# A fourth attention with four step banks, an opening in eight banks, and routed rows ranked before the router's turn

## The chip, the cores and the metric

The kernel runs on one core of one Trainium2 chip. The metric is the device time of one execution in microseconds. The kernel is written by hand for the five engines (TensorE, VectorE, ScalarE, GpSimd, SyncE); each has its own program, and they meet at semaphores.

## The reference

Four layers, each a cross attention and a feed-forward part, over `x` (16 batches of 100 tokens, 256 wide) with a context of 361 rows of 192 for every batch, all in float32:

```python
x = x + tanh(g_xattn[0]) * L0_xattn(ctx, layernorm(x), mask, ...)   # 4 heads of 64; keys and values of context and latents; q and k RMS-normed
x = x + tanh(g_ffn[0])   * L0_ffn(layernorm(x), ...)                # top-1 of 8 experts, 256 -> 2x1024 -> 256
x = x + tanh(g_xattn[1]) * L1_xattn(layernorm(x), ctx, ...)         # 8 heads of 64
x = x + tanh(g_ffn[1])   * L1_ffn(layernorm(x), ...)
x = x + tanh(g_xattn[2]) * L2_xattn(layernorm(x), ctx, ...)         # 4 heads of 64
x = x + tanh(g_ffn[2])   * L2_ffn(layernorm(x), ...)
x = x + tanh(g_xattn[3]) * L3_xattn(layernorm(x), ctx, ...)         # one head of 256, layer norms on both sides
x = x + tanh(g_ffn[3])   * L3_ffn(layernorm(x), ...)                # slots
```

The router of the first feed-forward picks one expert for every row: the kernel counts each row's rank among the rows of its expert, writes the rows to memory sorted by expert, and runs 20 tiles of 128 rows.

## The kernel before

The work goes in phases, attention and feed-forward in turn; within an attention the batches are pipelined. Every engine's program lists the same steps by hand in its own order, and an engine works strictly in that order.

PSUM has eight banks of 512 columns. In an attention, `S_bank` (banks 0, 1) takes scores, `PT_bank` (2, 3) the probabilities turned, `O_bank` (4) their products with the values, `R_bank` (5) the output turned, its projection and the router's small products, and `J_bank` (6, 7) the steps that prepare a later batch: turns and projections of context and x. A step is a group of matmuls by TensorE into a bank (raising `proj`), and a copy of the bank into SBUF by ScalarE (raising `copied`). TensorE's step n waits until the copy of the step two places before is done, since that one used the same bank.

**First attention (L = 0).** Twelve steps a batch. 0 and 1 turn the context's norms, 2 turns x, (5, 6) and (7, 11) are pairs that project the context to keys and values, 4 and 3 project x, 8 and 9 turn the keys and 10 the queries. 8, 9 and 10 need the keys and queries scaled by their root mean square: VectorE sums the squares (L1615, L1619, function `rms`), GpSimd takes the power and multiplies (L928, L933), five blocks a batch. Before the loop the opening prepares batches 0 and 1: batch 0's nine steps of `ALONE`, then those of batch 1 mixed with 8, 9, 10 of batch 0. `order_of` numbers these steps, `parity_of` gives the bank of two. ScalarE copies in that order, as its own list says. Then `first_attend(t)` runs for every batch, with steps for t+1 and t+2 between its own scores, turns and products. In it TensorE calls `o_turn(t-1)` (turn of the output, then `router_turn` of t-2), later `pair_blocks` of the pair (5, 6) of t+2, then the turns of the probabilities (`probs_turn`), and `project(t-1)` (projection, router logits, and `router_ranks` of t-3: two products, one for the ranks within the batch, L2348, one for the counts, L2349). VectorE reads ranks and counts in `residual` after `out`.

**Fourth attention (L = 3).** One head; four steps a batch: 0 turns x, 1 and 2 turn the context's two halves, 3 projects x. They alternate over banks 6 and 7; scores and probabilities alternate over banks 0, 1 and 2, 3 by batch. `fourth_attend(t)` on TensorE: scores of t, `o_turn(t-1)`, steps 0, 1, 2 of t+1, `project(t-1)` with the turn of the mixture's norms of t-2 (L2355), `probs_turn(t)`, step 3 of t+1, `weigh(t)`. ScalarE: `o_copy(t-1)` (L1129), copy of step 0 (L1061), exponential of t (L1118), copies of 1, 2 (L1065) and 3 (L1069). VectorE: maximum of t (L1637), statistics of x of t+2, copy of the turned probabilities (L1646), residual of t-1, x norm of t+2, `o_scale(t)` (L1656), norm for the mixture. SyncE loads the context norms of a batch twice (288 KB each), with the slot weights of the last phase between.

Lines of TensorE: L2444 context turn and L2442 the same in the fourth attention, L2450 x turn, L2406 and L2414 the two parts of a pair, L2456 projections of x, L2473 and L2476 turns of keys and queries, L2522 and L2518 scores, L2533 turns of the probabilities, L2554 products with the values, L2563 output turn, L2573 projection, L2334 router turn. L1073 is ScalarE's copy of steps 0 and 1 in the first attention, L1575 VectorE's context norm.

## Time and profile before

| | us |
|---|---|
| time, median of 3 runs | 1630.54 |
| lowest, highest | 1622.14, 1632.22 |
| the profiled execution's own time | 1626.69 |
| its span, first to last instruction | 1624.8 |
| TensorE busy | 1497.7 (92%) |
| TensorE weight load busy | 1087.5 (67%) |
| VectorE busy | 898.7 (55%) |
| ScalarE busy | 606.4 (37%) |
| GpSimd busy | 291.1 (18%) |

The profile is of one execution. PE is TensorE's matmul, PEld its weight load, DVE is VectorE, ACT ScalarE, POOL GpSimd, SP SyncE. A row of the timeline may merge equal instructions that follow each other (x4); its second number is the time from the first one's start to the last one's end. In brackets stands the idle time of the engine just before, and what ended it. Neighbouring matmuls overlap a little. PEclk is the granted TensorE clock, 1.00 for 2.4 GHz and 0.50 for 1.2.

### The profile page before, as it was taken

Reading aid. Unit: us, or ns where it says so; the run is one execution under the profiler, and the core shown is the slowest. Engines: PE = TensorE matmul, PEld = TensorE weight load, DVE = VectorE, ACT = ScalarE, POOL = GpSimd, SP = SyncE. Lnnn points to the kernel's source line nnn. Section 1 sums busy time; section 2 is a strip of 40 time slices with the busy share of each in tenths; the row PEclk is TensorE's granted clock in tenths of the full one; section 3 lists DMA queues with packets and bytes.
Section 4 is the critical chain, followed back from the end, with each engine's and each line's share of the span. In section 5 each row is a group of like instructions: output and inputs, shape, how many; then the busy total and the mean of one; then the engine's idle time right before and its main releaser. Section 6 shows DMA issues by size and latency. Waiting matters only on the chain.

```text
span 1624.8 us, 30316 instructions
## 1 busy us (share of the span) xinstructions
PE 1497.7 (92%) x9070; PEld 1087.5 (67%) x9070; DVE 898.7 (55%) x2901; ACT 606.4 (37%) x1704; POOL 291.1 (18%) x409
## 2 busy tenths in 40 slices
PE   5999999869999989999999989979999899878897
PEld 2566666559999956777677766747777644556665
DVE  4788788642222224555445444556666556556776
ACT  3655555412223323444434424304434100454342
POOL 4555556430000040000000000110000001121000
PEclk9999999959999999999999999989999899999898
DMA  5111114338999940000000000011100100243001
GB/s 138 32 34 37 36 36 155 118 122 299 324 329 320 327 127 15 20 18 18 18 9 18 10 1 10 17 41 30 37 27 27 33 13 20 65 148 100 1 11 31
DMA packets 89654, 128.85 MB, mean 79 GB/s; under 512 B 17362, under 2 KB 74786, under 8 KB 84450
## 3 DMA queue, kind: packets, MB, share of 16 engines
q1 hardware_dynamic: 85954, 123.50, 23.7%
q0 software_dynamic: 2432, 4.34, 0.9%
q8 instruction: 39, 0.64, 0.2%
q14 instruction: 45, 0.37, 0.1%
q10 hardware_dynamic: 1184, 0.01, 0.0%
HBM read 112.87 MB, written 11.67 MB: 77 GB/s over the span
## 4 chain that ended last, share of the span: by engine, by line
PE 75%; issue 8%; DVE 7%; POOL 3%; DMA 3%; ACT 3%; SPq 1%; ACTq 0%; POOLq 0%; DVEq 0%
PE bank L2406 10%; PE bank L2554 9%; PE bank L2763 7%; PE bank L2414 6%; PE bank L2856 6%; PE bank L2522 5%; PE bank L2533 4%; PE bank L2573 4%; PE bank L2777 4%; PE bank L2809 3%; PE bank L2825 3%; PE bank L2495 2%; PE bank L3007 2%; DMA work<-in_F_b1c 1%; PE bank L2456 1%
## 5 line engine op out<-in xcount | busy, mean ns | idle before, releaser
L1646 DVE COPY work<-bank 128x300 f32<-128x300 f32 (+1 forms) x272 | 124.0, 489 | 144.5 <-PE bank L2533 143.2
L2554 PEld LDWEIGHTS bank<-work 128*100 128x100 f32 x1760 | 177.1, 171 | 34.0 <-issue 19.1
L2554 PE MATMUL bank<-work 128*100 128x64 f32 (+1 forms) x1760 | 191.5, 260 | 9.1 <-DVE work L1646 7.2
L1118 ACT ACTIVATE work<-bank,work 100x361 f32<-100x361 f32 (+1 forms) x272 | 158.7, 590 | 52.3 <-DVE work L1637 36.2
L1981 DVE SCALAR_TENSOR_TENSOR work<-bank,work 128x128 f32<-128x128 f32 x160 | 56.1, 350 | 160.4 <-PE bank L2763 148.5
L2763 PE MATMUL bank<-work 128*128 128x128 f32 x1216 | 142.7, 275 | 0.7 <-DMA work<-in_F_b1c 0.5
L2763 PEld LDWEIGHTS bank<-work 128*128 128x128 f32 x1216 | 140.5, 192 | 2.2 <-ACT work L1239 1.2
L1637 DVE TENSOR_REDUCE work<-bank 100x1 f32<-100x361 f32 x208 | 102.0, 528 | 68.7 <-PE bank L2522 66.1
L2533 PEld LDWEIGHTS bank<-ident,work 100*128 100x128 f32 x880 | 91.7, 144 | 43.0 <-issue 22.8
L2533 PE MATMUL bank<-ident,work 100*128 100x100 f32 x880 | 107.3, 256 | 7.1 <-ACT work L1118 6.6
L1239 ACT ACTIVATE work<-bank,work 128x128 f32<-128x128 f32 x160 | 58.7, 367 | 143.7 <-PE bank L2763 138.7
L2522 PE MATMUL bank<-work 64*100 64x361 f32 (+1 forms) x512 | 110.2, 508 | 0.6 <-ACT work L1102 0.6
L1108 ACT COPY work<-bank 128x512 f32<-128x512 f32 (+2 forms) x96 | 41.3, 482 | 154.0 <-PE bank L2414 154.0
L906 POOL TENSOR_TENSOR work<-work,neg_half 100x1 f32<-100x1 f32 x64 | 35.2, 550 | 331.1 <-DVE work L1595 296.2
L2856 PE MATMUL bank<-F_weight,work 128*128 128x512 f32 (+1 forms) x208 | 92.3, 603 | 0.0
L928 POOL TENSOR_TENSOR work<-work,neg_half 128x4 f32<-128x4 f32 x80 | 82.0, 1024 | 42.2 <-DVE work L1619 42.1
L865 POOL TENSOR_TENSOR work<-work,neg_half 100x1 f32<-100x1 f32 x48 | 28.1, 586 | 296.3 <-DVE work L1503 270.2
L1105 ACT COPY work<-bank 128x361 f32<-128x361 f32 x96 | 39.5, 464 | 96.5 <-PE bank L2414 96.5
L2777 PE MATMUL bank<-work 128*128 128x256 f32 x320 | 72.5, 380 | 0.5 <-DVE work L1981 0.5
L2856 PEld LDWEIGHTS bank<-F_weight,work 128*128 128x128 f32 (+1 forms) x208 | 39.1, 190 | 49.0 <-issue 39.7
L2777 PEld LDWEIGHTS bank<-work 128*128 128x128 f32 x320 | 59.3, 190 | 7.8 <-DVE work L1981 0.7
L2406 PE MATMUL bank<-L_WkvT,work 128*128 128x512 f32 (+1 forms) x128 | 50.6, 518 | 14.2 <-ACT work L1073 13.5
(390 smaller groups left out, 2754.5 us busy)
## 6 DMA issues: line engine op xcount, KB each, us to landing
work<-in_F_w SPq DMA_DIRECT2D x58, 1024.0 KB, 5.7
work<-in_ctxT SPq DMA_DIRECT2D x64, 180.5 KB, 2.4
work<-context_norms SPq DMA_DIRECT2D x32, 288.0 KB, 3.5
context_norms<-work SPq DMA_DIRECT2D x16, 288.0 KB, 2.5
work<-in_ctx SPq DMA_DIRECT2D x16, 192.0 KB, 2.9
work<-in_F_b SPq DMA_DIRECT2D x20, 128.0 KB, 6.4
work<-sorted_x SPq DMA_DIRECT2D x20, 128.0 KB, 2.6
sorted_y<-work SPq DMA_DIRECT2D x20, 128.0 KB, 5.9
```

The lines of the kernel that those rows point to most:

```text
L928: nc.gpsimd.tensor_tensor(rr[j][:, 4 * k:4 * k + 4], rr[j][:, 4 * k:4 * k + 4], neg_half[:, 0:4], ALU.pow).then_inc(s.rqk.sem, 1)
L1118: nc.scalar.activation(pr[:, 0:NK], S_bank[k][0:T, 0:NK], ACT.Exp, bias=nmax[k][0:T, :], accum_out=rsum[j][0:T, h:h + 1]).then_inc(s.exped ...
L1637: nc.vector.tensor_reduce(nmax[k][0:T, :], S_bank[k][0:T, 0:NK], axis=AXX, op=ALU.max, negate=True).then_inc(s.maxed.sem, 1)
L1646: nc.vector.tensor_copy(PT[k][:, 0:CH, :], PT_bank[k][:, 0:CH * T].rearrange("p (c t) -> p c t", c=CH)).then_inc(s.probs_copied.sem, 1)
L2406: nc.tensor.matmul(to, lhs, rhs, start=(i == 0), stop=False, skip_group_check=True)
L2414: ins = nc.tensor.matmul(to, lhs, rhs, start=False, stop=True, skip_group_check=True)
L2522: ins = nc.tensor.matmul(S_bank[k][0:T, 0:NK], QT[j][b:b + W, m, :], kt(L, j)[b:b + W, m, 0:NK], start=True, stop=True)
L2533: ins = nc.tensor.transpose(PT_bank[k][:, c * T:(c + 1) * T], PR[k][0:T, c, :], ident[0:T, 0:T])
L2554: ins = nc.tensor.matmul(to, PT[k][:, c, :], values, start=(c == 0), stop=(c == CH - 1))
L2763: ins = nc.tensor.matmul(bank[to + f % 2][:, 0:P], first_weights(i, j)[:, c, col:col + P], TT[j][:, c, :], start=(c == 0), stop=(c == 1))
L2777: ins = nc.tensor.matmul(bank[6 + j][:, 0:D], AC[j][:, f, :], W2[j][:, f, :], start=(f == 0), stop=(f == HID0 // P - 1))
L2856: ins = nc.tensor.matmul(bank[3 + q % Y_BANKS][0:k, :], GXT[:, c, i * P:i * P + k], lin2[:, c, 2 * g:2 * g + 2, :].rearrange("p e n -> p ( ...
```

## The change

Three parts.

The opening's nineteen steps are listed in `OPENING`, in their order; step k goes to bank (6 + k) mod 8, and waits for the copy seven places before. TensorE turns x of batch 0 before the first pair, and batch 1's context between the projections of batch 0's x. Two steps of the opening, the pair (7, 11) of batch 1, keep their places and banks 7 and 6.

In the fourth attention the steps 0 to 3 have banks 6, 7, 1 and 3; scores are always in bank 0 and turned probabilities in bank 2. A step waits only for the copy of the same step of the batch before. Step 1 of t+1 goes ahead of `o_turn(t-1)`, so ScalarE's copy of step 0 waits for the first two steps.

`router_ranks` goes from the end of `project` into `o_turn`, ahead of `router_turn`.

```diff
+OPENING = ((0, 0), (0, 1), (0, 2), (0, 5), (0, 6), (0, 4), (1, 0), (1, 1), (0, 3), (0, 7), (0, 11), (1, 2), (1, 5), (1, 6),
+           (0, 8), (1, 4), (1, 3), (0, 9), (0, 10))
...
+def opens(t, n):
+
+    return isinstance(t, int) and (t, n) in OPENING
+
+
+def reused_after(t, n):
+
+    return order_of(t, n) - (7 if opens(t, n) else 1)
+
+
 def order_of(t, n):
 
+    if opens(t, n):
+        return OPENING.index((t, n))
...
+        def ahead_bank(t, n):
+            return bank[(6 + order_of(t, n)) % 8] if opens(t, n) else J_bank[parity_of(t, n)]
...
             if L == 3 and isinstance(t, int) and t == 0:
                 return S_bank[n % 2]
+            if L == 3:
+                return (bank[6], bank[7], bank[1], bank[3])[n]
...
                         src = step_bank(L, t, j, n)
-                        wait_for(act, s.proj, STEPS[L] * t + place_of(L, t, n) + 1)
+                        wait_for(act, s.proj, STEPS[L] * t + (2 if L == 3 and n < 2 else place_of(L, t, n) + 1))
...
-                    for n in ALONE:
-                        step(0, 0, n)
                     act.wait_ge(loaded["head_gains"], 16 * n_loads["head_gains"])
...
-                    for n in AHEAD[:-2]:
-                        step(*((0, 0) if n in OF_NEXT else (1, 1)), n)
+                    for t, n in OPENING:
+                        step(t, t, n)
...
-                        wait_for(pe, s.copied, STEPS[L] * t + place - 1)
+                        if L == 3 and not (isinstance(t, int) and t == 0):
+                            wait_for(pe, s.copied, STEPS[L] * (t - 1) + n + 1)
+                        else:
+                            wait_for(pe, s.copied, STEPS[L] * t + place - 1)
...
                     if PAIRS[L] == 0:
-                        wait_for(pe, s.exped, n - 1)
+                        wait_for(pe, s.exped, n)
...
-                    wait_for(pe, s.probs_copied, n - 1)
+                    wait_for(pe, s.probs_copied, n if L == 3 else n - 1)
...
+                    if L == 0 and not (isinstance(t, int) and t < 2):
+                        router_ranks(t - 2, R_bank)
                     if L == 0 and not (isinstance(t, int) and t == 0):
                         ins = router_turn(t - 1, slot)
...
                         ins = router_logits()
-                    if L == 0 and not (isinstance(t, int) and t < 2):
-                        ins = router_ranks(t - 2, R_bank)
...
                     scores(t, j, 0)
+                    if more:
+                        step(t + 1, 1 - j, 1)
                     if started:
                         o_turn(t - 1, 1 - j)
-                    for n in (0, 1, 2):
+                    for n in (0, 2):
...
                     step(0, 0, 0)
                     step(0, 0, 1)
+                    step(0, 0, 2)
                     pe.wait_ge(loaded["wkv"], 16 * n_loads["wkv"])
                     pair_blocks(0, 0, FIRST_PAIRS[0])
                     pair_rests(0, 0, FIRST_PAIRS[0])
-                    step(0, 0, 2)
                     pe.wait_ge(loaded["wlkv"], 16 * n_loads["wlkv"])
                     step(0, 0, 4)
+                    step(1, 1, 0)
+                    step(1, 1, 1)
                     step(0, 0, 3)
                     pair_blocks(0, 0, FIRST_PAIRS[1])
                     pair_rests(0, 0, FIRST_PAIRS[1])
-                    step(1, 1, 0)
-                    step(1, 1, 1)
+                    step(1, 1, 2)
                     pair_blocks(1, 1, FIRST_PAIRS[0])
                     pair_rests(1, 1, FIRST_PAIRS[0])
-                    step(1, 1, 2)
                     step(0, 0, 8)
                     step(1, 1, 4)
                     step(1, 1, 3)
```

## Rows read from the trace of the kernel before

**Rows 1.** Busy time by stretches: start and end, length, each engine, PEclk, DMA share, GB/s

```profile
18.12:42.55 24.43, 18.03 (x57) 8.81 (x56) 11.29 (x42) 11.92 (x36) 15.09 (x21) 0.86 0.38 97
60.00:332.00 272.00, 252.85 (x1607) 170.67 (x1604) 214.21 (x832) 150.43 (x414) 145.52 (x184) 0.98 0.22 67
1391.60:1513.50 121.90, 97.36 (x575) 71.64 (x575) 68.90 (x225) 57.05 (x155) 24.36 (x45) 0.94 0.34 103
```

**Rows 2.** Waits of TensorE, whole run: total us, times, longest

```profile
PE bank L2442 <- ACT work L1061: 15.5, 15, 1.1
PE bank L2406 <- ACT work L1073: 13.5, 16, 2.2
```

**Rows 3.** Timeline of the opening and of the first loop step, in order of time

```profile
12.36 3.75 PE L2406 MATMUL bank<-L_WkvT,work 128*128 128x512 f32 x4 [2.17 <-ACT work L1073]
...
16.04 2.08 PE L2414 MATMUL bank<-L_WkvT,work 64*128 64x512 f32 x4
...
18.40 0.96 DVE L1575 TENSOR_SCALAR work<-work 128x192 f32<-128x192 f32 x3 [0.17 <-POOL work L900]
...
20.70 2.94 PE L2456 MATMUL bank<-L_WlkvT,work 128*128 128x512 f32 x4 [1.17 <-ACT work L1077]
20.81 1.02 POOL L928 TENSOR_TENSOR work<-work,neg_half 128x4 f32<-128x4 f32 x1 [1.93 <-DVE work L1619]
...
22.47 1.01 POOL L928 TENSOR_TENSOR work<-work,neg_half 128x4 f32<-128x4 f32 x1
...
34.88 0.88 PE L2473 MATMUL bank<-ident,work 128*128 128x128 f32 x4 [0.44 <-ACT work L1083]
...
41.49 1.13 PE L2406 MATMUL bank<-L_WkvT,work 128*128 128x256 f32 x4 [0.46 <-ACT work L1093]
...
52.77 1.88 PE L2456 MATMUL bank<-L_WlkvT,work 128*128 128x512 f32 x4
...
54.49 1.03 PE L2456 MATMUL bank<-L_WqT,work 128*100 128x256 f32 x4
```

**Rows 4.** First attention: timeline of a batch, and TensorE's waits from 66 to 350 us

```profile
104.50 0.32 PE L2348 MATMUL bank<-work,earlier 100*100 100x8 f32 x2
...
104.90 0.37 PE L2450 MATMUL bank<-ident,work 100*128 100x100 f32 x2
...
117.17 1.98 PE L2406 MATMUL bank<-L_WkvT,work 128*128 128x512 f32 x4 [0.65 <-ACT work L1073]
...
PE bank L2406 <- ACT work L1073: 8.2, 12, 0.7
...
PE bank L2533 <- ACT work L1118: 4.6, 5, 1.5
```

**Rows 5.** Fourth attention: timeline of two batches, and the context norms' loads

```profile
1428.50 0.38 PE L2563 MATMUL bank<-ident,work 100*96 100x100 f32 x2 [0.24 <-DVE work L1656]
...
1428.92 0.75 ACT L1129 ACTIVATE work<-bank,L_ln_b,L_ln_g 96x100 f32<-96x100 f32 x2 [2.65 <-PE bank L2563]
...
1430.21 0.56 ACT L1118 ACTIVATE work<-bank,work 100x361 f32<-100x361 f32 x1
...
1430.46 0.51 PE L2442 MATMUL bank<-ident,work 128*96 128x128 f32 x3 [1.04 <-ACT work L1061]
...
1430.81 1.03 PE L2573 MATMUL bank<-L_Wv,work 96*100 96x256 f32 x4
...
1432.39 0.47 DVE L1646 COPY work<-bank 128x300 f32<-128x300 f32 x1 [2.37 <-PE bank L2533]
...
1434.13 1.38 PE L2518 MATMUL bank<-work 96*100 96x361 f32 x4
...
1435.89 0.37 PE L2563 MATMUL bank<-ident,work 100*96 100x100 f32 x2 [0.38 <-DVE work L1656]
...
1444.74 0.38 PE L2563 MATMUL bank<-ident,work 100*96 100x100 f32 x2 [0.24 <-DVE work L1656]
...
work<-context_norms SPq DMA_DIRECT2D x28, 288.0 KB, 3.3
```

More of the change, by code:

```diff
@@ L135, in raised_by_attention @@
     return counts
+def opens(t, n):
+    return isinstance(t, int) and (t, n) in OPENING
+def reused_after(t, n):
+    return order_of(t, n) - (7 if opens(t, n) else 1)
 def order_of(t, n):
+    if opens(t, n):
+        return OPENING.index((t, n))
     if n not in OF_NEXT:
-        return ALONE.index(n) if isinstance(t, int) and t == 0 else 9 + 12 * (t - 1) + AHEAD.index(n)
+        return 9 + 12 * (t - 1) + AHEAD.index(n)
     return 9 + 12 * t + (n - 8 if isinstance(t, int) and t == B - 1 else AHEAD.index(n))
@@ L1050, in step @@
                     if L == 0:
-                        src = J_bank[parity_of(t, n)]
+                        src = ahead_bank(t, n)
                         wait_for(act, s.proj, order_of(t, n) + 1)
@@ L1628, in maximum @@
                             wait_for(dve, s.mask_row, t + 1)
-                        sc = S_bank[k][0:T, 0:NK]
+                        sc = S_bank[0 if L == 3 else k][0:T, 0:NK]
                         apart(dve)
@@ L1636, in maximum @@
                     else:
-                        nc.vector.tensor_reduce(nmax[k][0:T, :], S_bank[k][0:T, 0:NK], axis=AXX, op=ALU.max,
+                        nc.vector.tensor_reduce(nmax[k][0:T, :], S_bank[0 if L == 3 else k][0:T, 0:NK], axis=AXX, op=ALU.max,
                                                 negate=True).then_inc(s.maxed.sem, 1)
@@ L1645, in probs_copy @@
                     wait_for(dve, s.pv, n - 1)
-                    nc.vector.tensor_copy(PT[k][:, 0:CH, :], PT_bank[k][:, 0:CH * T].rearrange("p (c t) -> p c t", c=CH)
+                    nc.vector.tensor_copy(PT[k][:, 0:CH, :], PT_bank[0 if L == 3 else k][:, 0:CH * T].rearrange("p (c t) -> p c t", c=CH)
                                           ).then_inc(s.probs_copied.sem, 1)
@@ L2377, in part_of @@
                         cols = slice(0, 512) if n in FIRST_PAIRS[0] else slice(D * r, D * (r + 1))
-                        return ((J_bank[parity_of(t, n)][:, 0:cols.stop - cols.start], CT[j][lo:hi, c, keys:keys + P],
+                        return ((ahead_bank(t, n)[:, 0:cols.stop - cols.start], CT[j][lo:hi, c, keys:keys + P],
                                  wkv0[lo:hi, c, cols]),)
@@ L2396, in pair_blocks @@
                         if L == 0:
-                            wait_for(pe, s.copied, order_of(t, n) - 1)
+                            wait_for(pe, s.copied, reused_after(t, n))
                             if n == 5:
@@ L2421, in step @@
                     if L == 0:
-                        dst = J_bank[parity_of(t, n)]
-                        wait_for(pe, s.copied, order_of(t, n) - 1)
+                        dst = ahead_bank(t, n)
+                        wait_for(pe, s.copied, reused_after(t, n))
                     else:
@@ L2500, in scores @@
                     n = H * t + h
-                    k = (H * j + h) % 2
+                    k = 0 if L == 3 else h % 2
                     if PAIRS[L] == 0:
-                        wait_for(pe, s.exped, n - 1)
+                        wait_for(pe, s.exped, n)
                     elif h % 2 == 0:
@@ L2521, in scores @@
                         m, b = h // 2, W * (h % 2)
-                        ins = nc.tensor.matmul(S_bank[k][0:T, 0:NK], QT[j][b:b + W, m, :], kt(L, j)[b:b + W, m, 0:NK],
+                        ins = nc.tensor.matmul(S_bank[0 if L == 3 else k][0:T, 0:NK], QT[j][b:b + W, m, :], kt(L, j)[b:b + W, m, 0:NK],
                                                start=True, stop=True)
```

6 lines of the change are left out of this document (3 added, 3 removed).

## The prediction, made before the changed kernel was run

> **What bounds the kernel now.** I read the busy time by stretches first [rows 1]. In the first attention TensorE is busy 252.85 of 272 us at granted clock 0.98: there a microsecond of TensorE idleness removed is a microsecond of the stage. In the fourth attention it is busy 97.36 of 121.90 us (80%), with no other engine near that (VectorE 68.90), so the stage is a chain of hand-overs. In the opening, from the end of the first pair of products to the first attend, it is busy 18.03 of 24.43 us at granted clock 0.86. The list of TensorE's waits over the whole run names two of the three places that the change touches: 15.5 us in 15 waits of L2442 (a context turn of the fourth attention) on ScalarE's L1061, and 13.5 us in 16 waits of L2406 (the pair products) on L1073 [rows 2]. The third place, the opening, is a row of single waits on copies out of two banks [rows 3].
>
> **Opening.** The same instructions run in another order, in eight banks, so a step waits for the copy of seven steps back, not of two. TensorE's first pair runs from 12.36 to 18.12 us (3.75 and 2.08) [rows 3]; it waits for the copy of the context turn, and stays. Then, before, come idle times for the x turn and its copy, up to the start of (0,4) at 20.70. After, (0,2) has been turned and copied under the first pair, and (0,4) starts at 18.1. (1,0) and (1,1) need the norms of batch 1, whose L1575 ends at 18.40+0.96 = 19.4; (0,4) takes 1.88 at full speed (the row at 52.77), to 20.0, so they don't wait. (0,3) 1.03, the pair (7,11) and the pair (1;5,6) follow, and TensorE reaches (0,8) near 26. There it is late no more: (0,8) needs all five q/k blocks scaled by GpSimd, whose calls begin at 20.81 and 22.47, a step of 1.66. Five steps from 20.81 end at 20.81+5x1.66 = 29.1. GpSimd takes the place of the copies. From 29.1: (0,8) 0.9 (row at 34.88), (1,4) 1.9, (1,3) 1.0, (0,9) 0.9, (0,10) 0.4 (two turns, as the L2563 rows of 0.38), together 5.1, to 34.2. The last pair waits for ScalarE to empty (0,9), some 0.4: 34.6, against 41.49 before. That is 6.9 us. TensorE has now a wait of 3 us before (0,8), and if half speed follows it, (1,4) and (1,3) cost up to 2.9 more. I take 6.5; the ends are 3 (half speed, and another copy late) and 8 (GpSimd starts earlier). In the first attend I see nothing that gives it back: GpSimd's norms of batch 2 stand right behind the five steps, from 29.1, and are needed after 35; its scalings of batch 1 follow copies that come as much earlier. The weights awaited there (part 1) may land late; no row of mine bounds that, and the lower end of 3 is to hold it.
>
> A word on speed. The first pair ran at half the speed of later ones (3.75 us for four products of 512 columns, against 1.88 for the four at 52.77), that is at 1.2 GHz where the later ones had 2.4. (0,4) at 20.70 took 2.94 against 1.88 at 52.77.
> The Trainium skill, TensorE: Matmul & The Clock Gate, Part 1, says that the array starts throttled, that activity releases it and idleness brings it back; the trace agrees in direction, with the slow first pair and the slow (0,4) that comes after an idle stretch. By that rule the change, which takes idle time away, also takes slow stretches away: the fifth case below.
>
> **Ranks.** Two small products, L2348 and L2349 (two passes each), go from the end of project to the middle of o_turn. They hold TensorE 104.90-104.50 = 0.40 us [rows 4]. In o_turn they fall just before the wait of L2406 on L1073 (0.65 us at 117.17; 8.2 us in 12 waits over the steady part), which hides them; project is shorter by 0.40. So a batch gains 0.40 where the wait is there: eleven attends (batches 3 to 13) both have ranks and a pair to wait with, 4.4 us. But after the pair TensorE sometimes waits for the exponential too (4.6 us, 5 times [rows 4]); there the gain is lost, which leaves some seven, 3 us. The ends are 0 (all lost to the exponential) and 4.4. The ranks wait for the one-hot of batch t-3, made by VectorE a whole attend earlier: no wait. What is queued behind them is the router turn and then ScalarE's o_copy, later by 0.4, but that copy stands behind two exponentials and is not awaited until after the third and fourth scores. In the drain the chain o_turn, copy, project keeps its length.
>
> **Fourth attention.** Before, the second context turn waits for the bank that x turn filled, whose copy stands behind o_copy on ScalarE. In the batch from 1428.50 [rows 5]: o_turn 1428.50; o_copy (L1129) 1428.92 to 1429.67, so project could start at about 1429.8; but L2442 waits 1.04 us, to 1430.46, and project starts at 1430.81. One microsecond is lost in the chain. After, each step has its bank and none of these waits is left. From o_turn to the copy of the probabilities (L1646, 1432.39) it took 3.89; after, 1.3 to project, plus 1432.39-1430.81 = 1.58, is 2.9. The exponential is next: L1118 begins 1.71 after o_turn and takes 0.56, ready at 2.3 to 2.4, just when TensorE comes to turn it (2.34). From there to the next o_turn it took 3.50 (1432.39 to 1435.89), set by VectorE, whose residual, norms and o_scale are back to back; nothing in the change shortens this. TensorE's scores (1434.13, 1.38) end at 1435.51, and the context turn now put ahead of o_turn (0.5) ends at 1436.0, 0.1 past the old start: it fills the wait for o_scale (0.38) and costs 0.1. Net 3.89-2.9-0.1 = 0.9; I take 0.8, because the exponential is that near. Fifteen batches: 12 us. Ends: 0.3 each (exponential late, since the x copy now waits for two turns), 4.5; and all idleness gone, 1.04+0.38 = 1.4 each, 21. One bank for scores and one for turned probabilities cost nothing: TensorE has by then waited for the exponential and the copy in order to turn and weigh. The moved step waits for its DMA with o_turn queued behind it. A context load is issued some batch ahead and landed in 3.3 us in the median of the stage [rows 5], half a batch; where it shares the engines with a 768 KB slot weight it may be late once, a microsecond.
>
> **Sum.** 6.5+3+12 = 21.5 us. The profiled execution took 1626.69 us (span 1624.8), 3.85 below the median of 1630.54. From the first, 1605; carried to the median, 1630.5-21.5 = 1609.
>
> **The rivals.**
> (B) The fourth attention gains a third: ScalarE's queue (o_copy, x copy, exponential) becomes the chain. For: the exponential is ready only 0.1 us before need. Against: o_copy itself moves by only 0.1. 0.3x15 = 4.5 in place of 12: 14 in all, 1616.5.
> (C) The opening is given back: TensorE comes early into the first attend, but GpSimd and VectorE don't, and most of 6.5 goes. For: GpSimd is busy 15.09 of 24.43 us [rows 1]. Against: its calls follow copies that come earlier too. 15 to 16 us left, 1615.
> (D) The ranks do not do what they say: the wait of L2406 is set by ScalarE, and the 0.4 us reappear in front of the probabilities' turn. 18.5, 1612.
> (E) Fewer slow stretches. The batch from 1435.89 to 1444.74 took 8.85 us against 7.39 for the one before; its matmuls ran slowly after the wait. Stretches like it cost 1.5 each, and (0,4) and others in the opening some 3 together. If they vanish, 6 more: 27.5, 1603.
> (F) The other side: the speed of TensorE falls instead. Each fourth-attention batch pays the 1.46 us of that slow batch (15x1.46 = 22), and the opening runs at half speed from 18.1: its work there is 18.03x0.86 = 15.5 us at full speed, 14.5 up to the last pair; at half that is 29, to 47, so 5.5 later than 41.49 and not 6.5 earlier. +22-12+5.5-3 = +12.5: 1643. It is slower than before as soon as ten more batches than now run slow with the opening slow too. For: the dip came while TensorE was busy four fifths of the time. Against: waits get shorter.
> The Trainium skill, same page, A second HAM failure mode: psum-queue depth-cycling, speaks for F: going round through PSUM banks left TensorE many tiny idle times and its clock swinging. No run here shows it yet; the two-bank kernel before has such dips as well.
>
> **How the numbers follow.** Chances: forecast 0.50, B 0.12, C 0.12, D 0.08, E 0.14, F 0.04. The bounds of the terms give 7.5 to 33 together; not all fall on one end, so 12 to 31 from 1630.5 with F left out: 1599 to 1619. A measurement of this kernel can tell about 1% (16.3 us, 1614.2) from no change. Forecast, D and E lie nearly whole below that, B and C mostly above: faster 0.70, within 1% 0.27, slower 0.03.
>
> **What would show it.** Right: L2442's wait on L1061 is gone from the waits, and o_turn to o_turn falls from 7.39 to about 6.6; the busy share of TensorE there rises from 80% to near 90%; the wait left is on L1656 or L1118. L2406's wait on L1073 falls from 0.65 to about 0.25 in the batches with ranks. The last pair of the opening starts near 34.6, with one wait, before (0,8), put down to GpSimd's scaling (L933). Wrong: a new wait of L2442 on the context DMA, or of L2533 on L1118 of half a microsecond in each batch; a pair that starts near 38; a granted clock below 0.86 in the opening.

## The result, and the profile after

The changed kernel takes 1607.85 us (median of four runs, 1603.31 to 1612.29), the kernel before beside it 1629.19; the ratio is 0.9885, with a 95% interval of 0.9855 to 0.9914. In a second comparison it was 1609.79 against 1626.02, ratio 0.9904 [0.9889, 0.9919]. Forecast were 1609.0 us, and 21.5 us less. The sum was right; of its three terms the largest was right, the two others were too high, and some 6 us of what was gained stood in no term: they are stretches in which TensorE ran at half speed before and not after.

TensorE's waits over the whole run of the changed kernel (total us, times, longest); L2423 answers to L2406 of [rows 2], and L2442 of before is L2462 now:

```profile
PE bank L2423 <- ACT work L1092: 12.1, 15, 6.1
...
PE bank L2574 <- DVE work L1663: 10.8, 14, 3.2
...
PE bank L2553 <- ACT work L1137: 7.3, 10, 1.1
PE bank L2595 <- ACT work L1148: 6.4, 16, 0.8
...
PE bank L2493 <- POOL work L952: 2.1, 1, 2.1
```

The 15.5 us of L2442 on L1061 are gone. The pair products still wait 12.1 us, but 6.1 of them are one wait, the first: before, the longest was 2.2. And a wait on GpSimd has come (L2493), as forecast. L2595 on L1148, 6.4 us in 16 waits, is the projection of the fourth attention's output on ScalarE's copy (L1129 before): the wait that is left there, where the prediction had named VectorE's scaling or the exponential.

Where the time went is read best from marks that both kernels pass, TensorE's first or last instruction of a kind. Each number is the length of a stage in one profile, in us:

| stage | before | before, again | after | after, again | all_three |
|---|---|---|---|---|---|
| start to the opening's last pair | 41.5 | 42.4 | 36.3 | 38.0 | 31.2 |
| from there to the first attention's last pair | 262.4 | 263.0 | 262.4 | 261.1 | 261.3 |
| drain: from there to the last router logits | 42.2 | 42.2 | 38.6 | 36.0 | 38.5 |
| feed-forwards, second and third attention | 1045.5 | 1045.5 | 1046.4 | 1046.0 | 1046.4 |
| fourth attention, to the first slot product | 121.9 | 120.3 | 107.9 | 106.5 | 101.1 |
| slot phase, to the end | 111.3 | 115.3 | 109.8 | 118.1 | 109.9 |
| span | 1624.8 | 1628.7 | 1601.4 | 1605.7 | 1588.4 |

(all_three is the last kernel of the experiments.) Before to after, in the first pair of profiles: -5.2, 0, -3.6, +0.9, -14.0, -1.5, together -23.4. In the second pair: -4.4, -1.9, -6.2, +0.5, -13.8, +2.8, together -23.0. So the fourth attention's gain and most of the opening's repeat; the rest is spread otherwise in each execution, and the table says how far one profile can be trusted for a term of 3 us.

### The profile page after: what moved, and what is told of

Read it like the earlier page. It is cut to its first block, busy times and chain, and to the rows that moved or that the text cites. A ratio compares the mean times of both kernels' runs of the same rounds, so it can differ in the third digit from the quotient of the medians.

```text
span 1601.4 us, 30303 instructions
## 1 busy us (share of the span) xinstructions
PE 1487.3 (93%) x9070; PEld 1080.0 (67%) x9070; DVE 898.4 (56%) x2901; ACT 606.8 (38%) x1704; POOL 291.5 (18%) x409
## 4 chain that ended last, share of the span: by engine, by line
PE 71%; issue 9%; POOL 7%; DVE 6%; DMA 3%; ACT 2%; SPq 1%; POOLq 0%; ACTq 0%; DVEq 0%
PE bank L2423 9%; PE bank L2574 8%; PE bank L2785 7%; PE bank L2878 6%; PE bank L2431 5%; PE bank L2542 5%; PE bank L2595 4%; PE bank L2553 4%; PE bank L2799 4%; PE bank L2831 3%; PE bank L2847 3%; POOL work L947 3%; PE bank L2515 2%; PE bank L3029 2%; DMA work<-in_F_b1c 2%
## 5 line engine op out<-in xcount | busy, mean ns | idle before, releaser
L1124 ACT COPY work<-bank 128x361 f32<-128x361 f32 x96 | 39.5, 465 | 96.4 <-PE bank L2431 96.4
L2542 PEld LDWEIGHTS bank<-work 64*100 64x100 f32 x512 | 42.5, 166 | 29.4 <-issue 15.0
```

The lines of the kernel that those rows point to most:

```text
L2542: ins = nc.tensor.matmul(S_bank[0 if L == 3 else k][0:T, 0:NK], QT[j][b:b + W, m, :], kt(L, j)[b:b + W, m, 0:NK], start=True, stop=True)
```

## The experiments

**One part at a time.** Three kernels, each the kernel before with one of the three parts of the change, and one with the whole change less one detail.

ranks_alone:

```diff
@@ def o_turn
+                    if L == 0 and not (isinstance(t, int) and t < 2):
+                        router_ranks(t - 2, R_bank)
@@ def project
-                    if L == 0 and not (isinstance(t, int) and t < 2):
-                        ins = router_ranks(t - 2, R_bank)
```

> The kernel before, with only the rank products moved from project into o_turn. Theory of the prediction: L2406's wait on L1073 falls from 8.2 to about 4 us in the first attention and the time of the stretch from the last opening pair to the last pair product (261.9 us before) falls by 3. Rival: the wait falls, but TensorE then waits longer for VectorE's copy of the probabilities (2.0 to about 5.6 us, as in the changed kernel), and the stretch falls by less than 1 us; 1629 within noise.

fourth_alone:

```diff
+            if L == 3:
+                return (bank[6], bank[7], bank[1], bank[3])[n]
...
-                    k = (H * j + h) % 2
+                    k = 0 if L == 3 else h % 2
...
@@ def fourth_attend
                     scores(t, j, 0)
+                    if more:
+                        step(t + 1, 1 - j, 1)
...
-                    for n in (0, 1, 2):
+                    for n in (0, 2):
```

> The kernel before, with only the fourth attention's four step banks, single score and probability banks and the step ahead of o_turn. Theory: period 6.5 us in place of 7.38, the fourth attention (first scores to first slot product) falls from 121.9 to about 109 us, total 12 to 14 less than before, about 1616. Rival: part of the 14 us seen between the same marks in the changed kernel was a slow stretch of TensorE that was absent there by chance; then 10 to 12.

opening_alone:

```diff
+OPENING = ((0, 0), (0, 1), (0, 2), (0, 5), (0, 6), (0, 4), (1, 0), (1, 1), (0, 3), (0, 7), (0, 11), (1, 2), (1, 5), (1, 6),
...
+    return order_of(t, n) - (7 if opens(t, n) else 1)
...
+            return bank[(6 + order_of(t, n)) % 8] if opens(t, n) else J_bank[parity_of(t, n)]
```

> The kernel before, with only the opening in eight banks and its order (ScalarE's early wait for the head gains with it). Theory: the last opening pair starts at 36.3 in place of 41.5, and all of the 5.2 us stay until the end: about 1624. Rival: the first attention gives part of it back, its stretch grows from 261.9 and the total is within 2 us of before.

Measured, as ratios to the kernel before on the same chip (median 1625.98 us of its runs there):

| kernel | median us | ratio | 95% interval |
|---|---|---|---|
| ranks_alone | 1621.95 | 0.9984 | 0.9960 to 1.0008 |
| fourth_alone | 1617.14 | 0.9929 | 0.9891 to 0.9968 |
| opening_alone | 1625.97 | 0.9987 | 0.9960 to 1.0013 |
| gains_wait_late | 1607.71 | 0.9872 | 0.9833 to 0.9911 |

By the medians alone the parts give 4, 9 and 0 us, 13 of the 21. By the stage that each part touches they give more: the opening's last pair starts at 36.3 us in opening_alone (41.4 in fourth_alone, 40.0 in ranks_alone), the fourth attention lasts 106.6 us in fourth_alone (121.7 in ranks_alone, 120.0 in opening_alone), the drain 39.6 us in ranks_alone (42.2 in the other two). In the profiled executions what hides them is the slot phase, which no part touches: 117.9 us in fourth_alone and 118.2 in opening_alone, 109.8 in ranks_alone. Whether the same holds for the executions behind the medians, which have no profile, is not shown. A single part of 5 us can't be told by the time of a kernel whose last phase lasts anything from 109.8 to 118.2 us; its stage tells it.

The 40.0 us of ranks_alone, whose opening has the same steps in the same order as before, says something of the 41.5 too. The four products of (1,4) took 3.43 us at 35.62 in the kernel before, the same in fourth_alone (3.44) and before_again (3.48), but 1.96 and 1.95 in the two profiles of ranks_alone. So 1.5 of the 5.2 us between 41.5 and 36.3 is one half-speed stretch that the order before need not have; against 40.0 the new order gains 3.7. Why ranks_alone lacks the stretch is not shown.

**The opening's wait for the head gains.** I had missed one edit: ScalarE's wait for the head gains and the scaling of q_gain, before between the ninth and the tenth of its opening steps, now stand ahead of all nineteen. ScalarE and TensorE of the changed kernel, timeline of the opening:

```profile
13.83 1.28 ACT L1222 ACT_TABLE_LOAD   x1 [13.83 <-DMA L_kn_g<-in_L_kn_g]
...
16.74 3.75 PE L2423 MATMUL bank<-L_WkvT,work 128*128 128x512 f32 x4 [6.09 <-ACT work L1092]
...
30.98 0.61 POOL L952 TENSOR_TENSOR work<-work 128x256 f32<-128x256 f32 x1
...
31.74 0.63 PE L2493 MATMUL bank<-ident,work 128*128 128x128 f32 x4 [2.13 <-POOL work L952]
32.21 1.88 PE L2476 MATMUL bank<-L_WlkvT,work 128*128 128x512 f32 x4
...
36.28 1.13 PE L2423 MATMUL bank<-L_WkvT,work 128*128 128x256 f32 x4 [0.71 <-ACT work L1112]
```

ScalarE does nothing until 13.83 us and is released by the load of the key gains; its first copy, which the first pair waits for, starts at 15.36 where it was 10.98 before, 4.4 us later, and the pair starts at 16.74 and not at 12.36 [rows 3]. The kernel gains_wait_late is the changed kernel with this wait behind the fourteenth step:

```diff
-                    act.wait_ge(loaded["head_gains"], 16 * n_loads["head_gains"])
-                    nc.scalar.mul(qg0s[:, :], q_gain[:, :], HWID[0] ** -0.5).then_inc(start.scaled, 1)
-                    act.wait_ge(start.scaled, 1)
-                    for t, n in OPENING:
+                    for k, (t, n) in enumerate(OPENING):
+                        if k == 14:
+                            act.wait_ge(loaded["head_gains"], 16 * n_loads["head_gains"])
+                            nc.scalar.mul(qg0s[:, :], q_gain[:, :], HWID[0] ** -0.5).then_inc(start.scaled, 1)
+                            act.wait_ge(start.scaled, 1)
```

> The changed kernel, with ScalarE's wait for the head gains put back behind the copies of the first fourteen opening steps (ahead of (0,8), the first that uses them). Theory: in the changed kernel this wait holds ScalarE until 13.83 us, the table load and the first copies follow, and TensorE's first pair starts at 16.74 instead of 12.36. The pair then starts near 12.4; GpSimd's five scalings then set the time of (0,8), first call near 20.8, fifth product done near 29.1 (31.6 in the changed kernel), and the last opening pair starts near 33.8 (36.28): 2.5 us less than the changed kernel in all. Rival: the first copies are late because the load of the gains or TensorE itself is late; then the pair stays near 16.7 and the time is the changed kernel's.

Its opening, the same view (its lines from L1222 on are one higher):

```profile
9.60 1.28 ACT L1092 ACT_TABLE_LOAD   x1 [9.60 <-PE bank L2465]
...
12.69 3.75 PE L2424 MATMUL bank<-L_WkvT,work 128*128 128x512 f32 x4 [2.22 <-ACT work L1092]
...
27.79 0.61 POOL L952 TENSOR_TENSOR work<-work 128x256 f32<-128x256 f32 x1
...
28.55 1.09 PE L2494 MATMUL bank<-ident,work 128*128 128x128 f32 x4 [2.14 <-POOL work L952]
29.43 3.06 PE L2477 MATMUL bank<-L_WlkvT,work 128*128 128x512 f32 x4
...
34.68 1.13 PE L2424 MATMUL bank<-L_WkvT,work 128*128 128x256 f32 x4 [0.72 <-ACT work L1112]
```

The first pair is back at 12.69, GpSimd ends its fifth scaling at 28.40 (31.59 in the changed kernel), and the last pair starts at 34.68. The prediction had 34.6 for the kernel as it read the diff, that is without this edit; two deviations of it cancel there, the scaling that ends 0.7 earlier than 29.1, and the stretch from (0,8) to the last pair, 6.1 us and not 5.5. Of the 4.05 us gained at the first pair 3.2 reach (0,8), and only 1.6 the last pair, because the products behind the wait for GpSimd ran at half speed here (3.06 us for the four that took 1.88 in the changed kernel). In the changed kernel's second profile they took 3.01 us too, and its last pair started at 38.0. The half-speed stretch belongs to the execution, then, and costs some 1.6 us when it falls there: from (0,8) to the last pair it is 6.13 and 6.08 us with it, 4.54 in the changed kernel's first profile without. Against 38.0, gains_wait_late is 3.3 us earlier.

**Filling the wait for GpSimd.** Blocks (1,4) and (1,3), which need nothing of GpSimd, go ahead of (0,8):

```diff
-           (0, 8), (1, 4), (1, 3), (0, 9), (0, 10))
+           (1, 4), (1, 3), (0, 8), (0, 9), (0, 10))
...
+                        if k == 16:
+                            act.wait_ge(loaded["head_gains"], 16 * n_loads["head_gains"])
...
-                    step(0, 0, 8)
                     step(1, 1, 4)
                     step(1, 1, 3)
+                    step(0, 0, 8)
```

> The changed kernel with ScalarE's wait for the head gains moved behind its sixteenth opening eviction (as in the run named gains_wait_late, whose last opening pair started at 34.68 us) and with blocks (1,4) and (1,3) of the opening ahead of (0,8), on TensorE and ScalarE alike. Theory A: in gains_wait_late TensorE waits 2.14 us at (0,8) for GpSimd's scaling chain, whose last piece lands at 28.4 us, and the products behind that wait go at half speed (3.06 us instead of 1.88 for the second); two blocks that wait for nothing of GpSimd fill it. Then no wait for L952 is left, and the last opening pair starts 2 to 3 us earlier, at 32 to 32.7 us. Rival: the last pair waits for something else, the evictions of ScalarE (0.71 us before it in both runs) or the loads of weights that (1,4) and (1,3) want; then it starts at 34 to 35 us and the new place of the wait shows it. The fourth attention keeps its period of 6.5 us, and the stage its 106 to 108 us.

TensorE's timeline from there on:

```profile
25.49 1.98 PE L2477 MATMUL bank<-L_WlkvT,work 128*128 128x512 f32 x4
27.31 1.03 PE L2477 MATMUL bank<-L_WqT,work 128*100 128x256 f32 x4
28.17 1.04 PE L2494 MATMUL bank<-ident,work 128*128 128x128 f32 x8
...
30.47 1.13 PE L2424 MATMUL bank<-L_WkvT,work 128*128 128x256 f32 x4 [1.09 <-ACT work L1112]
```

No wait for L952 is left: the turns of (0,8) and (0,9) run as eight in a row at 28.17, and the last pair starts at 30.47, 4.2 us before gains_wait_late's and more than the 2 to 3 expected. Not all of it is the edit's: 0.9 us lies ahead of the moved blocks, where the rests of the first pair (L2432) took 1.25 us here and 1.99 there. From the pair (1;5,6) to the last pair it is 7.88 us, in all_three too, against 11.23 in gains_wait_late and 9.64 in the changed kernel's first profile: the edit brings 3.4 us where half speed follows the wait and 1.8 where it does not (the wait of 2.14 less 0.38 more before the last pair). The gain reaches the end of the loop in part: its last pair rests start at 292.5 us against 295.7. The median is 1599.37 us, ratio 0.9823 [0.9777, 0.9869].

**What sets the period of the fourth attention.** One batch of the changed kernel, from the turn of its outputs to the next (TensorE, ScalarE and VectorE, in order of time):

```profile
1403.42 0.38 PE L2583 MATMUL bank<-ident,work 100*96 100x100 f32 x2
...
1404.64 1.11 PE L2595 MATMUL bank<-L_Wv,work 96*100 96x256 f32 x4 [0.34 <-ACT work L1148]
...
1405.13 0.56 ACT L1137 ACTIVATE work<-bank,work 100x361 f32<-100x361 f32 x1
...
1406.43 0.47 DVE L1663 COPY work<-bank 128x300 f32<-128x300 f32 x1 [1.49 <-PE bank L2553]
...
1408.85 0.41 DVE L1616 TENSOR_SCALAR work<-X,work 100x256 f32 x1
...
1409.37 0.42 DVE L1673 TENSOR_SCALAR work<-bank,work 100x192 f32<-100x192 f32 x1
1409.39 0.49 PE L2462 MATMUL bank<-ident,work 128*96 128x128 f32 x3
...
1409.93 0.37 PE L2583 MATMUL bank<-ident,work 100*96 100x100 f32 x2
```

6.51 us against 7.39 in [rows 5]. The projection comes 1.22 after the turn (2.31 before; the prediction said 1.3), VectorE's copy of the probabilities 1.79 later, and the next turn 3.50 after that copy, as before. Two things now stand within a tenth of a microsecond of each other ahead of the turn at 1409.93: VectorE's scaling (L1673) ends at 1409.79, and TensorE's own step ahead of the turn (L2462) at 1409.88. Three kernels take them apart. norm_after_scale moves VectorE's norm L1616 behind the scaling:

```diff
                         residual(t - 1, 1 - j)
+                    o_scale(t, j)
                     if two_more:
                         ln_x_norm(t + 2, j)
-                    o_scale(t, j)
```

> The changed kernel with one edit in VectorE's part of the fourth attention: the norm of x two batches ahead is issued behind the scaling of the heads' outputs of the present batch instead of ahead of it, so that the scaling is ready some 0.33 us earlier. Theory A, VectorE's chain from scores through maxima, exponential, scaling to the turn of the outputs sets the period of 6.50 us: the period falls to 6.2 us and the stage from 107.9 to about 103 us. Rival, TensorE's own order sets it (next batch's scores and its step 1 stand ahead of the turn of the outputs and end 0.1 us after the scaling is ready): the period stays at 6.4 to 6.5 us, the stage at 106.5 to 108 us.

step_behind_turn gives TensorE's step 1 its old place and keeps the banks:

```diff
-                    if more:
-                        step(t + 1, 1 - j, 1)
...
-                    for n in (0, 2):
+                    for n in (1, 0, 2):
```

> The changed kernel with step 1 of the next batch put back behind the turn of the outputs on TensorE in the fourth attention (order 1, 0, 2 behind it), the four banks kept. Theory A, VectorE's scaling releases the turn: the turn keeps its time, the step fills the 0.34 us in which TensorE waits for the turned outputs' copy before the projection, and the period stays at 6.5 us (6.4 to 6.6), the stage at 106 to 109 us: what the change brought is then the banks, not the order. Rival, the order matters: without the step ahead TensorE idles ahead of the turn and the period rises to 6.8 us or more, the stage to 113 us or more.

> The two edits of norm_after_scale and step_behind_turn together. If each of the two paths (VectorE's scaling; TensorE's scores and step ahead of the turn) ends within 0.1 us of the other in the changed kernel, neither edit alone brings anything and both together bring 0.3 to 0.35 us a batch: period 6.15 to 6.2 us, stage 102 to 103 us. Rival: the period is set by the sum of TensorE's work (some 5.8 us of 6.5 busy) with the waits for VectorE's maxima and probabilities, which neither edit moves; then it stays at 6.4 to 6.5 us.

The turns of the outputs, TensorE's timeline, in norm_after_scale:

```profile
1404.64 0.34 PE L2583 MATMUL bank<-ident,work 100*96 100x100 f32 x2
...
1411.03 0.34 PE L2583 MATMUL bank<-ident,work 100*96 100x100 f32 x2
```

in step_behind_turn:

```profile
1404.72 0.37 PE L2583 MATMUL bank<-ident,work 100*96 100x100 f32 x2 [0.23 <-DVE work L1673]
...
1411.22 0.38 PE L2583 MATMUL bank<-ident,work 100*96 100x100 f32 x2 [0.24 <-DVE work L1673]
```

and in both_fourth:

```profile
1403.92 0.37 PE L2583 MATMUL bank<-ident,work 100*96 100x100 f32 x2
...
1410.07 0.38 PE L2583 MATMUL bank<-ident,work 100*96 100x100 f32 x2
...
1416.24 0.37 PE L2583 MATMUL bank<-ident,work 100*96 100x100 f32 x2
```

| kernel | period, us | stage, us | median us | ratio |
|---|---|---|---|---|
| after (again) | 6.50 | 107.9 (106.5) | 1609.79 | 0.9904 [0.9889, 0.9919] |
| norm_after_scale | 6.39 | 104.9 | 1601.43 | 0.9857 [0.9814, 0.9899] |
| step_behind_turn | 6.50 | 106.1 | 1605.57 | 0.9875 [0.9834, 0.9915] |
| both_fourth | 6.16 | 101.0 | 1596.45 | 0.9820 [0.9779, 0.9861] |

Each edit alone brings 0.11 and 0.00 us a batch by the median of the intervals, both together 0.34: two paths of nearly one length, of which either holds the other up. (Four of norm_after_scale's fifteen intervals are 6.25 us, and one is 7.51, since a context load came 1.06 us late there.) The idle time before the turn says which path is last: none in the regular batches of the changed kernel and norm_after_scale, where TensorE's own step ends last, 0.24 us on L1673 in step_behind_turn, where VectorE's scaling does. In step_behind_turn the change's order is undone and its gain is all there, so what the change brought in this stage is the banks; and the reorder, which was to fill TensorE's wait for the scaling, stands in the way as soon as the scaling comes earlier.

**Adding up, and what repeats.** all_three is order_14_first's opening with both_fourth's fourth attention; beside it ran the changed kernel, the kernel before and ranks_alone once more.

> The opening of order_14_first and the fourth attention of both_fourth in one kernel. Theory: the two gains sit in different stages and add: (1,4) and (1,3) first took the last opening pair from 36.3 to 30.5 us and the last pair of the first attention from 298.7 to 292.5 us, the fourth stage fell from 107.9 to 101.0 us. So the stage marks are 292 to 293 us and 101 us again, and the median lies 10 to 13 us below the changed kernel's of the same call. Rival: the clock levels of the drain (36 to 42 us) and of the slot phase (110 or 118 us) fall otherwise with the moved start and take back 6 to 14 us, so that it lies within 6 us of the changed kernel.

> The changed kernel once more, for a comparison on the same chip as all_three. Theory that the granted clock of a stage belongs to the program and its phase: the drain of the first attention is 38.6 us at clock 0.79 again and the slot phase 109.8 us. Rival, that it belongs to the execution: the drain lies anywhere from 36 to 42 us and the slot phase at 110 or 118 us, with all steps ahead of them as before (first pair 16.74 us, period of the fourth 6.50 us).

> The kernel before once more. Three profiles without the ranks moved (before, fourth_alone, opening_alone) all had a drain of 42.2 us at clock 0.67, the ones with them 36.0 to 41.4 us. If the clock of the drain belongs to the program, it is 42.2 us again; if to the execution, another value between 36 and 42 us.

> The kernel with the ranks alone once more. Its first profile had a first attention of 262.0 us with TensorE busy 248.1 us (clock 0.99) and a drain of 39.6 us at 0.70. If the ranks' own gain in the loop is the 1.4 to 1.9 us that the profiles at clock 1.00 show (262.4 before; 261.0 and 260.5 in two kernels with the ranks), a profile without the slow stretch gives 260.5 to 261.0 us; if the slow stretch belongs to the program it is 262.0 us again. The drain is 39.6 us again by the one, 36 to 42 us by the other.

all_three takes 1591.12 us (1589.91 to 1594.06), ratio 0.9790 [0.9776, 0.9805] to the kernel before, and lies 18.7 us below the changed kernel's median of the same runs (0.9904 [0.9889, 0.9919]). Its stages are the expected ones (last pair at 31.2 us, the first attention's last pair at 292.5, fourth attention 101.1); 17.3 us, more than the 10 to 13 expected, lie between the two profiles since the slot phase was 109.9 us in the one and 118.1 in the other; for the medians, 18.7 us apart, no profile tells the phases. It beats both kernels.

The theory of a clock that belongs to the program fell: the same program had a drain of 38.6 and 36.0 us, and a slot phase of 109.8 and 118.1. The kernel before had 42.2 twice in the drain, ranks_alone 39.6 and 39.5 there and 262.0 and 261.7 in the loop, both with the slow stretch (TensorE busy 248.1 and 248.0 us, clock 0.99), so the 260.5 to 261.0 expected of an undisturbed profile did not come. (The 260.5 was itself read from a start 0.5 us late: both_fourth's last opening pair starts at 35.28, and its stretch is 261.0 us.)

## Why the prediction was right, point by point

**Opening: 6.5 forecast, 5.2 and 4.4 measured, 3.7 without a slow stretch of the kernel before.** The step that failed is "it waits for the copy of the context turn, and stays": the first pair did not stay at 12.36, it moved to 16.74, since I read the move of ScalarE's wait for the head gains as part of the loop's new order and gave its DMA no time. The rest held. GpSimd takes the place of the copies: its five steps have the pitch of 1.66 us, TensorE waits 2.13 us for L952 and for nothing else before it, and from (0,8) to the last pair it took 4.5 us (5.5 forecast). Without the missed edit the last pair starts at 34.68 against 34.6. The check that I had named (one wait, put down to GpSimd, before (0,8)) was met while the total was off by 1.7: a check on one place doesn't see a shift of everything ahead of it. And the sign of being wrong that I had named, a pair that starts near 38, did come in the second profile (38.00). The penalty of half speed behind the wait, put at up to 2.9, was some 1.6 in two of the seven profiles that have this wait and absent in five. What the change gains by its own order is less than 5.2: the kernel before had a half-speed stretch near 36 us in both its profiles that ranks_alone, with the same opening, has in neither, and it is worth 1.5.

**Ranks: 3 forecast; 1.4 in the loop, and in the drain, for which I had written none, some 1.0 by themselves.** TensorE's waits from the opening's last pair to the last one of the loop, before:

```profile
PE bank L2406 <- ACT work L1073: 10.2, 14, 1.1
...
PE bank L2554 <- DVE work L1646: 1.6, 2, 1.3
PE bank L2533 <- ACT work L1118: 1.3, 2, 1.0
```

and in ranks_alone:

```profile
PE bank L2406 <- ACT work L1073: 5.8, 13, 1.1
PE bank L2554 <- DVE work L1646: 3.3, 6, 1.4
...
PE bank L2533 <- ACT work L1118: 1.2, 2, 0.9
```

The pair's wait falls by 4.4 us, the eleven times 0.40 of the prediction, so the ranks do hide in it. What gives part back is not the exponential (L1118: 1.3 and 1.2), as I had it, but VectorE's copy of the turned probabilities (L1646), which now waits in six batches and not two: +1.7. That leaves 2.7. The stretch itself shrank by 0.4 only, since TensorE's busy time rose from 246.0 to 248.1 us there, at granted clock 0.99 and not 1.00. In profiles at 1.00 the loop lasts 262.4, 263.0, 262.4 and 263.0 us without the ranks moved (before, before_again, fourth_alone, opening_alone) and 261.1, 261.0, 261.4, 261.0, 261.6, 261.3 and 262.0 with them (after_again, gains_wait_late, norm_after_scale, both_fourth, step_behind_turn, all_three, order_14_first): the means are 262.7 and 261.3, 1.4 us apart.

"In the drain the chain o_turn, copy, project keeps its length" is the other step that failed. Busy time of the drain: start and end, length, TensorE, its weight load, VectorE, ScalarE, GpSimd, PEclk, DMA share, GB/s. Before:

```profile
303.90:346.10 42.20, 33.55 (x184) 24.65 (x182) 22.28 (x97) 10.32 (x26) 8.39 (x11) 0.67 0.05 13
```

ranks_alone:

```profile
302.00:341.60 39.60, 31.55 (x184) 23.68 (x182) 22.13 (x97) 10.33 (x26) 8.73 (x11) 0.70 0.06 16
```

both_fourth, whose drain has the changed kernel's program:

```profile
296.30:332.30 36.00, 25.45 (x184) 19.09 (x180) 21.86 (x96) 10.33 (x26) 8.74 (x11) 0.87 0.07 18
```

Part of the 2.6 us between the first two is the ranks themselves. The end of project, TensorE's timeline, before (L2341 is the router logits, L2554 the next weighing, L2334 the next router turn):

```profile
327.25 0.72 PE L2341 MATMUL bank<-F_router_w,work 128*100 128x8 f32 x4
...
328.58 2.91 PE L2554 MATMUL bank<-work 128*100 128x64 f32 x16
...
339.80 0.72 PE L2341 MATMUL bank<-F_router_w,work 128*100 128x8 f32 x4
...
344.52 0.60 PE L2334 MATMUL bank<-ident,work 100*128 100x100 f32 x2 [3.23 <-DVE work L1445]
```

and in ranks_alone:

```profile
323.53 0.72 PE L2341 MATMUL bank<-F_router_w,work 128*100 128x8 f32 x4
324.10 2.91 PE L2554 MATMUL bank<-work 128*100 128x64 f32 x16
...
336.04 0.72 PE L2341 MATMUL bank<-F_router_w,work 128*100 128x8 f32 x4
...
339.99 0.60 PE L2334 MATMUL bank<-ident,work 100*128 100x100 f32 x2 [3.23 <-DVE work L1445]
```

Where the ranks stood between the logits and what follows, 1.33 us become 0.57 and 4.72 become 3.95, at half speed; at the drain's first project, at full speed, 0.41 goes. In the last o_turn nothing hides them, and the way from the output's turn to its projection grows from 1.52 to 2.21. With 0.17 more of waiting elsewhere that is some 1.0 us net. The other 1.6 us lie in one place: in the profile before, TensorE runs at 1.2 GHz for some 3 us around 310 and ranks_alone has no such stretch there.

The rest of the gain is clock. TensorE runs the same 184 instructions in 33.55, 31.55 and 25.45 us, and is idle for 8.65, 8.05 and 10.55. In the profile before it is at 1.2 GHz from about 322 us, 18 us into the drain, to its end; in both_fourth from 323, which is 27 us into it, and at no time ahead of that. All four profiles without the ranks moved have a drain of 42.2 us at granted clock 0.67; the ten with them have 36.0 to 41.4 us at 0.70 to 0.87. That the drain runs at half speed for less of its time with the ranks moved is thus seen in two groups that don't overlap; why is not shown, and the same program gave 38.6 and 36.0.

**Fourth attention: 12 forecast, 14.0 and 13.8 measured, some 11.8 of it by the change's own chain.** The mechanism is as argued: L2442's wait on L1061 is gone, TensorE's busy share rose from 80% to 89%, the period fell from 7.39 to 6.50, the VectorE chain of 3.50 us is what is left, and the step ahead of the turn ends just behind the scaling. My working gave 0.9 a batch, and I took 0.8 for the nearness of the exponential; measured are 0.89. In the parts: the projection starts 1.22 us after the turn (1.3 forecast), but from there to VectorE's copy it took 1.79 and not 1.58, since the exponential starts 1.71 after the turn in both kernels and is now what TensorE's turn of the probabilities meets. That makes 3.01 where I had 2.9, and the next turn, forecast at 3.6 behind it with the 0.1 of the moved step, came at 3.50.

Slow batches have to be taken out first, from the starts of the turns of the outputs. Before, two batches took 8.71 and 8.85 us, in before_again 8.49 and 8.40, where the others took 7.38: 2.8 and 2.1 us in all. The changed kernel has none of these, but one interval of 7.05 in its first profile and one of 6.64 in its second, 0.55 and 0.14 us, at granted clock 1.00: there L2462, the step now ahead of the turn, waits 0.55 and 0.15 us for its context load. Without all of these the stage is 119.1 and 118.2 us before and 107.4 and 106.4 after: 11.7 and 11.8 less. The 15 intervals between turns give 12.3 of it (not 15 x 0.89 = 13.4, as the first is 0.71 and the last 0.09 shorter), and the stage's start takes 0.5 back. So the 12 was right for the chain, and the 2 on top are the two slow batches (2.8 and 2.1 us) less the late load. The moved step's load was late once, as the prediction had it, by 0.55 us where a microsecond was allowed (1.06 in norm_after_scale).

**The rivals.** B (a third of the fourth's gain) fell with the period. C (the opening given back in the loop) fell: opening_alone starts the loop at 36.3 against fourth_alone's 41.4, 5.1 us earlier, and ends it at 299.3 against 303.8, 4.5 earlier; 0.6 is lost, not most of it. D was right in part and wrong in its place: of the 4.4 us that the pair's wait fell by, 1.7 come back, not in front of the probabilities' turn but behind it, ahead of the weighing, as a wait on VectorE's copy. E, fewer slow stretches, is the part of the result that I had given 0.14 and no term in the sum: it adds 1.5 us in the opening, some 2.6 or 5.2 in the drain (3.6 or 6.2 less the ranks' own 1.0) and 2.8 or 2.1 in the fourth attention, and in the first profile takes 1.4 back in the loop. F fell: in the fourth attention the granted clock went from 0.94 and 0.96 to 0.97 and 0.99.

The sum came out right because an overlooked loss (the opening's 3.7 in place of 6.5) and a shortfall of the ranks (1.4 + 1.0 in place of 3) stand against what the clock gave in the opening, the drain and the fourth attention. That is luck within the range: by its own terms the change was worth 3.7 + 1.4 + 1.0 + 11.8, some 18 us.

## What to carry to other kernels

Where two hand-overs end within a tenth of a microsecond of each other, price an edit only together with its twin: alone each gave 0.0 and 0.11 us a batch, together 0.34. In a diff that rewrites the order of the opening, look at what is lifted over the loop as well as at what is in it, the waits for loads above all: one wait put ahead of the list cost 4.4 us at its head. And when a step is moved between two kernels' stages, compare stages at marks, in two profiles each; a phase that no edit touches moved the total by 8 us here.

## What the runs showed of the hardware that was not expected

The slot phase has lengths that differ by 8 us with the same instructions. Its beginning in the changed kernel, first profile and second (busy time by stretches):

```profile
1491.60:1499.60 8.00, 8.00 (x29) 4.88 (x30) 4.54 (x28) 1.99 (x4) 0.94 (x2) 0.79 0.00 0
```

```profile
1487.60:1495.60 8.00, 8.00 (x15) 4.41 (x16) 3.58 (x24) 1.39 (x3) 0.94 (x2) 0.50 0.00 0
1495.60:1605.70 110.10, 95.80 (x468) 67.53 (x467) 76.36 (x272) 37.24 (x121) 4.38 (x8) 0.92 0.05 16
```

The slot phase lasted 109.8 us in the first and 118.1 in the second. In its first eight microseconds, busy without a gap in both, the one starts 29 matmuls at granted clock 0.79 and the other 15 at 0.50, which is 1.2 GHz all through; the first kind of products (L2951) has a median of 500 ns in the one and 874 in the other. The rest of the phase has 0.96 in the one and 0.92 in the other, and 14 matmuls more at 0.28 us each are some 4 us; the other 4 of the 8.3 come of later slow stretches. In the twelve other profiles the phase began with a median of 500 ns in six and of over 870 in six, whatever was changed ahead of it (before with 500, before_again with 874). The Trainium skill, TensorE: Matmul & The Clock Gate, Part 1, says that the point of transition at a kernel's start varies from run to run and that for modelling the ramp is below 1% of a typical span. Here the half-speed stretches of one late phase differ by 8.3 us of 1605.7, 0.5% by themselves, and with the drain's 2.6 us between two profiles of one program they are as large as two of the three effects studied. The page and the trace agree on the variation, and 0.5% is within the page's 1%; that is no reason to leave it out of an account of 20 us.

Two more. The first pair of products runs at about half pace in every profile (3.74 or 3.75 us for four products of 512 columns in ten of the fourteen, 3.38 to 3.68 in the others, 1.88 later), also where TensorE was idle for 2.2 or for 6.1 us ahead of it. And the wait that the new opening has at (0,8), 2.1 us long, is followed by half speed in two of the seven profiles that have it (3.06 and 3.01 us for the four products, 1.88 in the other five): the price of a wait of that length is not one number but 2.1 or some 3.7 us.

On the rival F, the Trainium skill's section A second HAM failure mode: psum-queue depth-cycling, on the same page, tells of small idle times between groups in turning banks that make the clock swing. The change turns eight banks in the opening and four steps' banks in the fourth attention, and the clock of the latter rose (0.94 and 0.96 to 0.97 and 0.99), with two slow batches before and none after; what this kernel shows of that rule is only that more banks with less idle time between groups don't call it up.
